# Near keys over halves of 64 queries in 64x64 tiles of the array, one near unit per step, and round 1 ahead of the last far scores

## The reference, cut to what matters

```python
xn = layernorm(x)                          # x: (4, 2048, 256)
q, k, v = heads(xn @ q_w), heads(xn @ k_w), heads(xn @ v_w)   # 16 heads of 16
scores = (q * sigmoid(unity_scale)) @ k.T / 4
allowed = (j % 4 == 0) | (abs(i - j) <= 8)                    # STRIDE 4, LOCAL 8
attn = softmax(where(allowed, scores, -inf))
out = x + (attn @ v) @ o_w + o_b + fp8(xn) @ w8.T + bias
```

## Time and profile before

| | |
|---|---|
| median of 3 runs | 1085.3 us (1085.21 to 1086.64) |
| the profiled execution | 1086.0 us, its span 1084.2 us |
| PE, DVE, ACT, POOL busy | 1028.3, 933.8, 839.8, 251.2 us |
| granted clock of PE | 0.987 of full speed over the span |
| a step of the attention | 12.59 us in 45 of 63 intervals between `maximum`s, 12.76 on average |
| far reductions L1087 | 512 of 1,220 ns |
| exponentials L1028 and L1033 | 1,024 of 597 ns and 256 of 594 ns |
| near reductions L1090 | 128 of 1,023 ns |

### The profile page before, as it was taken

How to read it: one execution, slowest core, us unless ns; L and a number is a source line. 1 busy time by engine, 2 the same in 40 slices (tenths; PEclk the granted TensorE clock), 3 DMA queues, 4 the chain that set the end, 5 groups by cost and what they waited for, 6 DMA issues and landing times.

```text
span 1084.2 us, 27687 instructions
## 1 busy us (share of the span) xinstructions
PE 1028.3 (95%) x10694; PEld 462.7 (43%) x10695; DVE 933.8 (86%) x1162; ACT 839.8 (77%) x1590; POOL 251.2 (23%) x387
## 2 busy tenths in 40 slices
PE   4999999699999999999999999999999999999898
PEld 2666666233333333333333333333333333333487
DVE  6989897889999999999999999999999999999133
ACT  4667674288888888888888888888888888888600
POOL 2444453012212121221212122212121222212100
PEclk9999999599999999999999999999999999999999
DMA  6787878213223333333333333323343332231166
GB/s 197 227 254 252 262 250 274 54 46 88 85 83 90 98 85 93 102 91 99 97 96 109 98 99 95 104 84 108 91 113 88 105 91 82 86 85 58 48 236 239
DMA packets 166777, 134.07 MB, mean 124 GB/s; under 512 B 70492, under 2 KB 145884, under 8 KB 166636
## 3 DMA queue, kind: packets, MB, share of 16 engines
q1 hardware_dynamic: 163912, 128.06, 39.3%
q10 hardware_dynamic: 2736, 4.26, 1.2%
HBM read 71.13 MB, written 59.84 MB: 121 GB/s over the span
## 4 chain that ended last, share of the span: by engine, by line
PE 76%; DVE 12%; issue 7%; DMA 2%; ACT 2%; DVEq 0%; ACTq 0%
PE ps_attend L1228 17%; PE ps_attend L1145 12%; DVE peak_far L1087 10%; PE ps_attend L1186 10%; PE ps_project L621 7%; PE ps_attend L1235 6%; PE ps_attend L1308 5%; PE ps_attend L1156 4%; PE ps_project L679 4%; PE ps_attend L1197 3%; PE ps_project L594 3%; PE ps_attend L1163 3%; PE ps_attend L1204 2%; DMA sums<-out_rows 2%; PE ps_project L656 1%
## 5 line engine op out<-in xcount | busy, mean ns | idle before, releaser
L1087 DVE TENSOR_REDUCE peak_far<-ps_attend 128x2 f32<-128x1024 f32 x512 | 608.5, 1220 | 41.0 <-PE ps_attend L1186 30.8
L1028 ACT ACTIVATE probs<-ps_attend 128x512 f32<-128x512 f32 x1024 | 541.1, 597 | 49.5 <-PE ps_attend L1145 46.3
L1228 PE MATMUL ps_attend<-probs,v_op 128*17 128x512 f32 x2048 | 270.1, 600 | 0.5 <-issue 0.5
L1145 PE MATMUL ps_attend<-q_op,k_op 51*128 51x512 f16 x1024 | 252.1, 387 | 4.9 <-ACT probs L1028 3.3
L1186 PE MATMUL ps_attend<-k_op,q_op 48*128 48x512 f16 x1024 | 189.6, 388 | 26.1 <-DVE peak_far L1087 15.5
L1033 ACT ACTIVATE probs<-ps_attend 108x512 f32<-108x512 f32 x256 | 138.7, 594 | 34.6 <-PE ps_attend L1163 34.6
L1145 PEld LDWEIGHTS ps_attend<-q_op,k_op 51*128 51x128 f16 x1024 | 76.8, 93 | 193.9 <-ACT probs L1028 137.4
L894 POOL CAST negmax<-peak 128x16 bf16<-128x16 f32 x64 | 12.6, 196 | 609.6 <-DVE peak L1070 609.6
L1090 DVE TENSOR_REDUCE peak_near<-ps_attend 128x8 f32<-128x864 f32 x128 | 131.0, 1023 | 10.5 <-PE ps_attend L1204 10.4
L885 POOL TENSOR_TENSOR out_rows<-out_rows,share_rows 128x512 f32<-128x512 f32 x64 | 81.4, 1272 | 66.1 <-DMA share_rows<-shares_dram 64.0
L621 PE MATMUL ps_project<-xT_parts,w_parts 128*128 128x512 f16 x384 | 90.6, 387 | 2.1 <-DVE xT_parts L465 2.1
(11 more groups left out here) (91 smaller groups left out, 937.4 us busy)
## 6 DMA issues: line engine op xcount, KB each, us to landing
share_rows<-shares_dram SPq DMA_DIRECT2D x64, 256.0 KB
attn_dram<-out_rows SPq DMA_DIRECT2D x64, 256.0 KB, 5.5
q_dram<-qk_parts SPq DMA_DIRECT2D x48, 256.0 KB, 4.7
k_dram<-qk_parts SPq DMA_DIRECT2D x48, 256.0 KB, 2.7
q_op<-q_dram SPq DMA_DIRECT2D x128, 96.0 KB, 2.4
k_op<-k_dram SPq DMA_DIRECT2D x64, 144.0 KB, 3.1
v_dram<-v_sb SPq DMA_DIRECT2D x16, 544.0 KB, 3.0
base<-in_x SPq DMA_DIRECT2D x16, 512.0 KB, 4.7
```

The source lines that it names most:

```text
L1028: ins = nc.scalar.activation(probs[:, r, h], ps_s[st.bank(kind)], ACT.Exp, scale=undo)
L1087: ins = nc.vector.tensor_reduce(peak_far[:, :, p, tile], banks, AX_X, ALU.max)
L1145: nc.tensor.matmul(bank, k[half(f, KM), keys], q[half(f, KM), p], start=True, stop=True).then_inc(s_ready, 1)
L1228: ins = nc.tensor.matmul(ps_o[h * VW:h * VW + VR], v[:, r, h * VR:(h + 1) * VR], probs[:, r, h], start=(r == 0), stop=False)
```

## The change

**Halves of 64 queries.** Near keys are taken per half of 64 queries, whose window `NEAR` has 60 keys. A matmul has 48 or 51 rows and 60 to 64 columns of weights, and the two halves of queries (`sub`) and the two halves of partitions (`f`) go to four different 64x64 tiles of the array.
- `score_near` is called once per step: four mask matmuls of 512 columns, then 32 key matmuls of 64 columns into the same two banks. ACT takes two near exponentials instead of four.
- A step has one near unit instead of two: four mask matmuls of 480 columns and 32 key matmuls of 60. DVE reduces 128x960 elements once instead of 128x864 twice. `MAXIMA` has nine units, `AHEAD` is 4, so `maximum` comes after the four far units and the near unit right behind it.
- The near round has 32 matmuls of 64 columns instead of 16 of 128, each over 128 partitions; rows that belong to no key hold zeros in `v_op`, which POOL fills once (`v_zeroed`).
- The mask depends on the place in the window alone, so three small constants replace two long ones.

**Edges.** The 6 places at the ends of a key tile now hold copies of far keys: in one step per iteration (n = 2, 6, ... 58) POOL makes four copies (`set_edges`) behind the negmax parts, and PE's near unit of that step waits for them (`edges_ready`). The tile has its near keys at the ends and its far keys in the middle (`places`, `strided`).

**Values.** `load_v` has seven transfers instead of four per iteration, of 20 partitions each for near values, two to a piece.

**Order.** `near` and `near_unit` stand together behind the near round; `far_unit(1, 1)` and `far_unit(3, 0)` stand behind `maxima`; round 1 stands ahead of scores (3,0).

```diff
-AHEAD = 5
-TURN = 8
+AHEAD = 4
+TURN = 7
 MAXIMA = (
-    ("far", 2, 1), ("far", 1, 0), ("far", 0, 0), ("near", 0), ("far", 2, 0),
-    ("far", 3, 1), ("far", 1, 1), ("far", 3, 0), ("near", 1), ("far", 0, 1),
+    ("far", 2, 1), ("far", 1, 0), ("far", 0, 0), ("far", 2, 0),
+    ("near",), ("far", 3, 1), ("far", 1, 1), ("far", 3, 0), ("far", 0, 1),
 )
...
+        def set_edges(st):
+            k, it = k_op[st.parity(2)], st.iteration(2)
+            pool.wait_ge(k_loaded[st.parity(2)], 16 * 2 * 2 * PAIRS * (st.half_iteration(2) + 1))
+            edges = ((0, strided(0)), (SK - WPAD, strided(1)))
+            for i, (f, (to, of)) in enumerate(itertools.product(range(2), edges)):
+                nc.gpsimd.tensor_copy(k[half(f), to:to + WPAD], k[half(f), of:of + WPAD]).then_inc(edges_ready, 1)
+                pool.wait_ge(edges_ready, 4 * it + i + 1)
...
+            if st.n >= 0 and st.exists(2) and st.queries(2) == 0:
+                pool.wait_ge(negmax_ready, st.at(2))
+                set_edges(st)
...
-        def score_near(st, i):
+        def score_near(st):
             q, k = q_op[:, st.slot()], k_op[st.parity()]
-            banks = [free_score(st, ("near", 2 * i + f)) for f in range(2)]
...
+            banks = [free_score(st, ("near", f)) for f in range(2)]
+            for sub, f in itertools.product(range(2), range(2)):
+                nc.tensor.matmul(banks[f][half(sub, SUB)], near_one[half(f)], near_q[half(f)], start=True, stop=False)
+            for p, t in itertools.product(range(PAIRS), range(TT)):
+                for sub, f in itertools.product(range(2), range(2)):
+                    at = window(p, st.queries() * TT + t) + sub * SUB_STEP
+                    to = (p * TT + t) * SUB
+                    ins = nc.tensor.matmul(banks[f][half(sub, NEAR), to:to + SUB], k[half(f, KM), at:at + NEAR],
+                                           q[half(f, KM), p, t * P + sub * SUB:t * P + (sub + 1) * SUB], start=False,
+                                           stop=(p == PAIRS - 1 and t == TT - 1))
...
+            if st.queries(2) == 0:
+                pe.wait_ge(edges_ready, 4 * (st.iteration(2) + 1))
             if 2 * n + 2 > U_BANKS:
                 pe.wait_ge(u_used, 2 * n + 2 - U_BANKS)
...
-                to = v_op[par][r:WIN:STRIDE - 1, NS // P:, :]
+                sub, place = r // (STRIDE - 1), r % (STRIDE - 1)
+                to = v_op[par][sub * SUB + place:sub * SUB + NEAR:STRIDE - 1, NS // P + sub::2, :]
...
-                for t in tiles:
+                for t, sub in itertools.product(tiles, range(2)):
+                    block = NS // P + 2 * (st.queries(d) * TT + t) + sub
...
+                        at, to = (h // 2 * TT + t) * SUB, t * P + sub * SUB
+                        ins = nc.tensor.matmul(ps_o[h * VW:h * VW + VR, to:to + SUB], v[:, block, h * VR:(h + 1) * VR],
+                                               probs[:, r, h % 2, at:at + SUB], start=False,
...
             far(1, 0)
-            near_unit(0)
             far_unit(2, 0)
             far(1, 1)
             weigh_last(4)
-            near(0)
+            near()
+            near_unit()
             far_unit(3, 1)
-            far_unit(1, 1)
             far(2, 0)
             weigh_own(0)
             maxima()
+            far_unit(1, 1)
+            far_unit(3, 0)
             far(3, 1)
-            far_unit(3, 0)
-            near_unit(1)
+            weigh_own(1)
             far(3, 0)
-            weigh_own(1)
-            near(1)
             far_unit(0, 1)
```

More of the change, by code:

```diff
@@ L1210, in near_probs @@
-        def near_probs(h, t):
-            at = (t % 2 * PAIRS + h // 2) * P
-            return probs[0:WIN, ROUNDS - 1, t // 2 * 2 + h % 2, at:at + P]
+            for sub, f in itertools.product(range(2), range(2)):
+                nc.tensor.matmul(banks[f][half(sub, SUB), 0:PAIRS * TT * NEAR], near_q[half(f), 0:SUB],
+                                 near_k[half(f)],
+                                 start=True, stop=False)
+            for p, t in itertools.product(range(PAIRS), range(TT)):
+                for sub, f in itertools.product(range(2), range(2)):
+                    at = window(p, st.queries(2) * TT + t) + sub * SUB_STEP
+                    to = (p * TT + t) * NEAR
+                    ins = nc.tensor.matmul(banks[f][half(sub, SUB), to:to + NEAR],
+                                           q[half(f), p, t * P + sub * SUB:t * P + (sub + 1) * SUB],
+                                           k[half(f), at:at + NEAR], start=False,
+                                           stop=(p == PAIRS - 1 and t == TT - 1))
+                    if p == PAIRS - 1 and t == TT - 1 and sub == 1:
+                        ins.then_inc(u_ready, 1)
@@ L1223, in weigh @@
                 else:
[L1224 removed]
+                    nc.tensor.matmul(ps_o, keep["ident_bf"][:], near_q[:], start=True, stop=True)
             if r < ROUNDS - 1:
@@ L1244, in far_unit, with near_unit @@
                 unit(st, ("far", tile, p))
-            def near_unit(tiles):
-                unit(st, ("near", tiles))
+            def near_unit():
+                unit(st, ("near",))
             def far(r, p):
```

163 lines of the change are left out of this document (65 added, 98 removed).

## The result

| | before | change |
|---|---|---|
| median of the paired runs | 1085.8 us | 1102.9 us (1101.9 to 1103.2) |
| ratio, 95% interval | | 1.0155, 1.0138 to 1.0173 |
| span of the profiled execution | 1084.2 us | 1100.1 us |
| PE, DVE, ACT busy | 1028.3, 933.8, 839.8 us | 971.7, 867.9, 784.6 us |
| commonest step between `maximum`s | 12.59 | 12.49 |

PE, DVE and ACT have 55 to 66 us less to do each (POOL has 15 more), and the kernel is 17 us slower. The steps account for all of it: they grew by 16.6 and the span by 15.9, so the rest of the program gave 0.7 back. The 63 steps at the commonest length are 6.3 shorter (12.59 to 12.49); the 15 edge steps exceed that length by 28.0 where the same steps exceeded it by 5.3 before; the other 48 exceed it by 5.5 in all against 5.3. So -6.3 + 22.7 + 0.2.

What follows compares the result with a forecast made beforehand. The prediction took a ring of waits through DVE, PE's order and ACT's reads to bound each step. Ring -5.8, edges +22.5 and sums -3.5 gave +13.2, from the median of 1085.3 to 1098 us; range 1076 to 1120.

Steps and rivals of the forecast that it cites:

- The ring: Chain of waits through DVE, PE and ACT once round a step: 12.50 us against 12.59, -5.8 over 64 steps.
- 1.27: From DVE's start on far unit (3,0) until PE gets unit (2,1) out: 1.27 us.
- 2.37: On PE from weights round 2 to round 3, and from round 3 to the near round: 2.37 us each.
- 1.03: PE's near round, 16 groups of half the columns: 1.03 us, 1.00 before.
- 0.52: PE's near scores, masks and eight groups of four small matmuls at 0.035 each: 0.52 us.
- 0.78: From the near unit's start on PE until DVE starts on it: 0.78 us.
- 3.61: DVE from the near reduction back to (3,0), with (3,1), (1,1) and the reciprocal: 3.61 us.
- The edges: In 15 steps PE's near unit waits 1.50 us for POOL's four copies behind the negmax parts: +22.5 us.
- The sums: DVE's 7.1 us of waits for the sums in 8 steps, hidden or paid back: -7.1 to 0, middle -3.5.
- Round 1 ahead of scores (3,0): Moving this weights round on PE was put at 0, with 0.17 us to spare on the ring.
- Small tiles without overlap: Rival: the near scores' and near unit's small matmuls don't overlap their loads, 0.06 per group; 1119 us, chance 0.20.
- The rival that the work counts: Rival: DVE's idle time stays 0.77 per step, so less work gives steps of 11.71; 1048 us, chance 0.20.

Runs made afterwards that it cites:

- e6: Changed kernel with edges written early and the weights rounds and near unit moved among units and scores; ratio 0.9878 to the kernel before.
- e7: Changed kernel with edges written early and units, scores and rounds in a new order; ratio 0.9612 to the kernel before.
- e1: Changed kernel with the edges written before POOL waits for `maximum`; ratio 0.9989 to the kernel before.
- e4: Changed kernel with round 1 put back behind scores (3,0); ratio 1.0506 to the kernel before.
- e8: Kernel before with only round 1 moved ahead of scores (3,0); ratio 1.0494 to the kernel before.
- e12: e1 with the reciprocal in front of DVE's last unit, (0,1), instead of (3,0); ratio 0.9925 to the kernel before.
- e2: Changed kernel with the near unit ahead of the near scores, edges still late; ratio 1.0636 to the kernel before.
- e3: e1 with the near unit ahead of the near round; ratio 1.0273 to the kernel before.
- e5: e3 with unit (1,1) moved ahead of scores (2,0) and round 0; ratio 1.0169 to the kernel before.
- e10: e7 with the reciprocal in front of DVE's last unit and the two loads of heads issued two steps apart; 1014.4 us, ratio 0.9327 to the kernel before.

## Why the prediction was right

**The ring.** By its steps, predicted and measured: 1.27 and 1.21; 0.55 and 0.53; 2.37 and 2.38 twice; 1.03 and 1.02; 0.52 and 0.53; 0.78 and 0.84; 3.61 and 3.59. The two terms that are off by 0.06 cancel, which is luck: the first stood on a reduction that took 1.22, and (3,0) took 1.15; the second put 0.33 from the last group's start to DVE, and it took 0.38. The near scores' 0.52 was met in sum only: their groups start 0.030 apart and not 0.035, and from the last one to the near unit 0.09 passes. The sum, 12.50, met 12.49, and -5.8 met -6.3. It held because it was followed through the new order, not scaled from the work: the rival that scaled it gave 11.71, and e6 and e7 show that a length near it is there to be had (11.92, 11.57), but by another order.

**The edges.** 1.50 predicted, 1.66 measured (14.15 - 12.49), above the bound of 1.62. POOL's copies took 0.24 each with the wait for the one before, where 0.25 was put (917.77 to the last one's end at 918.69). The rest is what lies around them: the last copy ends at 918.69 and PE's first matmul is at 918.95; the prediction let the near unit start with the copies' end. e1 shows that the wait was POOL's place in the order alone: it is gone there, and with it 18 of the 22.7 us beyond the steps of before.

**The sums.** -3.5 was the middle of 0 and -7.1. The trace has the whole: none of the 7.1 is left in the steps, and with them went the 5.3 by which the edge steps of before exceeded the others. e1 shows that it is hidden under the edges' wait, as the prediction had it, since 5.7 of it comes back when that goes.

**What it left out.** In four of the edge steps another 0.74 to 1.01 is lost while PE has a lower granted clock (last section), 3.3 us in all. The prediction had 22.5 - 3.5 = +19.0 for edges and sums; the trace has +22.7, which is about 15 x 1.66 = 24.9 and this 3.3, less the 5.3. With the ring, +13.2 against +16.6 in the steps. So the range was met by the mechanism, and the 3.4 that are missing are the clock's 3.3, with the edges (2.4 too low) and the sums (1.8 too high) cancelling in the main.

**Round 1 ahead of scores (3,0)** was put at 0, for its ACT wait on the ring. In the sum that did no harm, because the ring had been followed with round 1 in its new place. As the price of the part alone 0 is wrong both ways: -0.70 per step in the change (e4), +0.87 in the kernel before (e8). A price was given to one move of several that only work together.

**The rivals.** Small tiles without overlap needed 0.06 per group of four. The near scores' eight groups go from 944.38 to 944.67 with the stretch to the near unit, 0.036 each; single records of the trace have the groups' starts 0.030 apart (944.377 to 944.587). Their 32 weight loads lie within 0.48 on the timeline of PE's weight loads, to the next mask's first:

```profile
944.16 0.52 PEld L1175 LDWEIGHTS ps_attend<-q_op,k_op 51*60 51x60 f16 x32
944.64 0.14 PEld L1206 LDWEIGHTS ps_attend<-near_k,near_q 48*64 48x64 bf16 x4
```

With 0.027 of a group taken by its columns, 0.003 is left for four loads of 0.10 to 0.11 each. The Trainium skill ("TensorE: Matmul & The Clock Gate", Part 3, The mechanism) lets a load overlap matmuls only in other row groups. By it the groups would pay for loads on their own rows; at most 0.003 each was paid, and the loads of the second group start at 944.378, beside the first group's matmuls on the same rows (944.377), so this trace differs from it. How the array does that, no run tells. The rival's time, 1119, lies 16 us over what was measured. One reading in the prediction's case for this rival was off: it says that no row has a shorter pitch than 0.06, but the near unit's pairs of 108 columns in the earlier trace rows go 0.05 apart (951.83 to 951.88), which spoke against the rival. The rival that the work counts asked for the near unit at DVE within 0.8 of `maximum`; it comes 1.78 behind (943.73 to 945.51), with DVE idle for 1.60 where the prediction's ring had 1.54.

## What to carry to other kernels

Where three engines are busy for over 85% of a step, follow the chain of releases once round the step in the new order and add it up; less work on the fullest engine comes back only if what it waits for moves too. Expect other loops close by: e12 found the next loop 0.08 under the first, and in e2, e3 and e5 one moved unit pushed another loop 0.26 to 0.38 above it. A small job on an idle engine is free only where nothing on that engine's queue stands in front of it: four copies of 0.24 cost 18 us behind the wait for `maximum`, and ahead of it PE no longer waits for them. Price the moves of a change together, and look for the order (which units between which rounds, where a transfer is waited for) before looking for less work: e10 does the same work as the change in 0.918 of its time.
